# Attention in two-unit pairs: one shared output tile, one copy and one division for two heads' groups

## The reference

```python
q = (x @ Wq + bq).reshape(B, T, H, D)
kv_latent = jax.nn.gelu(x @ Wkd + bkd, approximate=False)
lat = kv_latent[..., :L] + kv_latent[..., L:]
kv = lat @ Wku + bku
k = kv[..., :C].reshape(B, T, H, D)
v = kv[..., C:].reshape(B, T, H, D)
attn = jnp.einsum('bqhd,bkhd->bhqk', q, k) * (1.0 / math.sqrt(D))
attn = jnp.where(causal, attn, -jnp.inf)
attn = jax.nn.softmax(attn, axis=-1)
out = jnp.einsum('bhqk,bkhd->bqhd', attn, v).reshape(B, T, C)
return out @ Wo + bo
```

## Time and profile before

| | |
|---|---|
| runs | 657.80, 651.72, 657.49 us; median 657.49 |
| profiled execution | 652.23 us, its span 650.4 us |
| mean granted TensorE clock | 0.966 of full speed |
| busy share of the span | PE 91%, DVE 84%, ACT 75%, weight loads 67%, POOL 26% |

### The profile page before, as it was taken

One profiled execution on the slowest core, in us unless ns is written; L12 is line 12 of the kernel. 1 busy time (PEld: TensorE's weight loads), 2 busy tenths in 40 slices (PEclk: granted clock), 3 DMA queues, 4 the chain that ended last, 5 costly groups with the idle time before them and its releaser, 6 DMA issues.

```text
span 650.4 us, 10963 instructions
## 1 busy us (share of the span) xinstructions
PE 594.2 (91%) x3276; PEld 435.8 (67%) x3276; DVE 545.8 (84%) x1344; ACT 488.0 (75%) x860; POOL 167.8 (26%) x143
## 2 busy tenths in 40 slices
PE   8888889888999999999999999791998999999995
PEld 5465556555546688888888887350575788888884
DVE  3868888888858868988888887769898789999997
ACT  4648999999647899999999998697735566666663
POOL 4323223223304043554355433031432000000000
PEclk9789999999998999999999999996897899999999
DMA  7000000000100032102210200000000132222201
GB/s 250 1 1 2 2 3 1 1 0 1 34 1 0 18 150 98 75 24 98 97 74 23 97 24 1 1 25 1 0 1 1 35 125 89 90 89 90 89 1 65
DMA packets 6490, 28.81 MB, mean 44 GB/s; under 512 B 862, under 2 KB 990, under 8 KB 4383
## 3 DMA queue, kind: packets, MB, share of 16 engines
q1 hardware_dynamic: 6448, 28.32, 12.1%
HBM read 27.13 MB, written 1.19 MB: 44 GB/s over the span
## 4 chain that ended last, share of the span: by engine, by line
PE 61%; DVE 27%; ACT 5%; issue 5%; DMA 1%; POOL 0%; DVEq 0%; SPq 0%; ACTq 0%; POOLq 0%
PE PS L1192 16%; PE PS L1193 16%; PE PS L1194 16%; DVE STAT L865 9%; PE PS L1338 2%; PE PS L1293 2%; PE PS L1205 2%; DVE RA L885 2%; PE PS L1218 2%; DVE SU L891 1%; DVE HL L680 1%; PE PS L1307 1%; DVE HN L668 1%; ACT RA L617 1%; DVE AR L1151 1%
## 5 line engine op out<-in xcount | busy, mean ns | idle before, releaser
L1006 DVE TENSOR_TENSOR RA<-AR,RA 128x512 fp32r<-128x512 f32 x144 | 137.9, 980 | 27.4 <-ACT RA L516 25.9
L515 ACT ACTIVATE AR<-PS,BI 128x512 f32<-128x512 f32 x144 | 99.6, 691 | 17.9 <-PE PS L1194 10.5
L1192 PE MATMUL PS<-HH,WH 128*128 128x512 f32 x272 | 109.4, 402 | 0.1
L1194 PE MATMUL PS<-HL,WH 128*128 128x512 f32 x272 | 107.2, 394 | 0.0
L1193 PE MATMUL PS<-HH,WL 128*128 128x512 f32 x272 | 107.0, 394 | 0.0
L516 ACT ACTIVATE RA<-PS,BI 128x512 fp32r<-128x512 f32 x144 | 98.6, 685 | 0.0
L865 DVE CUSTOM_DVE_ANT_0 STAT<-PS,MQ 128x128 f32<-128x128 f32 (+1 forms) x256 | 76.3, 354 | 20.0 <-PE PS L1294 19.9
L1192 PE MATMUL PS<-RA,WH 128*128 128x512 f32 x208 | 82.4, 396 | 3.2 <-DVE RA L1158 2.0
L1193 PE MATMUL PS<-RA,WL 128*128 128x512 f32 x208 | 81.0, 389 | 0.0
L1194 PE MATMUL PS<-RA,WH 128*128 128x512 f32 x208 | 81.0, 389 | 0.0
L313 POOL TENSOR_TENSOR AR<-AR 128x512 f32<-128x512 f32 x32 | 51.1, 1597 | 112.1 <-DVE AR L818 112.1
(11 more groups left out here) (212 smaller groups left out, 1165.8 us busy)
## 6 DMA issues: line engine op xcount, KB each, us to landing
AR<-comb SPq DMA_DIRECT2D x15, 1024.0 KB, 4.7
WS<-in_w SPq DMA_DIRECT2D x9, 512.0 KB, 5.5
WS<-in_w SPq DMA_DIRECT2D x8, 384.0 KB, 3.0
M<-in_mats SPq DMA_DIRECT2D x1, 1384.0 KB, 10.9
X<-in_xT SPq DMA_DIRECT2D x4, 256.0 KB, 4.2
out_xT<-X SPq DMA_DIRECT2D x4, 256.0 KB, 2.1
AR<-in_wmod SPq DMA_DIRECT2D x1, 768.0 KB, 8.1
KM<-in_kmats SPq DMA_DIRECT2D x1, 162.5 KB
```

The source lines that it names most:

```text
L515: act.activation(G[:, c, :], PS[:, c, :], ACT.Gelu_apprx_tanh, bias=bias).then_inc(s["act"], 1)
L1006: dve.tensor_tensor(out=GL[:, m0 % 2, c, :], in0=G[:, c, :], in1=f(GH[:, m0 % 2, c, :]), op=ALU.subtract).then_inc(s["lo"], 1)
L1192: pe.matmul(out, wh, xh, start=first, stop=False)
L1194: return pe.matmul(out, wh, xl, start=False, stop=last)
```

## The change

Units go in pairs, `pair = n // 2`. The even unit's `values` starts the accumulation in the head's 32 rows. The odd unit's uses a window of the value tile that begins eight columns earlier (`- 8 * odd`), so that its output lands in rows 8 to 15 and its sum in row 24, and accumulates onto the same tile. `evac_out`, `spread_sum`, `recip` and `divide` run once for each pair, with the same 128x256 shapes. `ON` and `Wo` have two groups for four, so that `out_proj` is two matmuls for four. `PR` has four buffers for two; `LAT`, `VALL`, `PR` move in `AR`. The input `mats` shrinks from 1384 to 1256 KB.

The steps are ordered anew. `values` runs for unit `n-2` in place of `n-1`; in even steps it stands where it stood, at the end. In odd steps `values(n-2)` and `project(n+3)` change places. ACT's copy of a pair stands behind `exps(n)` of an odd step, its `recip` in the next even one. DVE has `spread_sum` in even steps and `divide` in odd ones.

```diff
-            def evac_out(n, n0):
-                act.wait_ge(pv_done, n + 1)
-                if n0 >= 2:
-                    act.wait_ge(on_done, n - 1)
+            def evac_out(pair, pair0):
+                act.wait_ge(pv_done, 2 * pair + 2)
+                if pair0 >= 2:
+                    act.wait_ge(on_done, pair - 1)
...
-                if n0 >= 2:
-                    evac_out(n - 2, n0 - 2)
                 exps(n, n0)
+                if n0 >= 3 and n0 % 2 == 1:
+                    evac_out((n0 - 3) // 2 + 4 * it, (n0 - 3) // 2)
                 if n0 + 3 < UNITS:
                     evac_proj(n + 3, (n0 + 3) % 4)
-                if n0 >= 2:
-                    recip(n - 2, n0 - 2)
+                if n0 >= 4 and n0 % 2 == 0:
+                    recip((n0 - 4) // 2 + 4 * it, (n0 - 4) // 2)
...
-                dve.stream_shuffle(SU[:, n0 % 2, :], OT[:, n0 % 2, :], [16] * 32).then_inc(su_done, 1)
+                dve.stream_shuffle(SU[:, pair0 % 2, :], OT[:, pair0 % 2, :], ([16] * 8 + [24] * 8) * 2)\
+                   .then_inc(su_done, 1)
...
-                if n0 >= 3:
-                    divide(n - 3, n0 - 3, it)
-                if n0 >= 2:
-                    spread_sum(n - 2, n0 - 2)
+                if n0 >= 4 and n0 % 2 == 0:
+                    spread_sum((n0 - 4) // 2 + 4 * it, (n0 - 4) // 2)
+                if n0 >= 5 and n0 % 2 == 1:
+                    divide((n0 - 5) // 2 + 4 * it, (n0 - 5) // 2, it)
...
-                if n0 >= 1:
-                    pe.wait_ge(ot_done, n)
-                if n0 + 2 < UNITS:
-                    pe.wait_ge(qm_ready, n + 3)
-                own = [slice(32 * (4 * (n0 % 4) + j), 32 * (4 * (n0 % 4) + j) + 32) for j in range(4)]
+                odd = n0 % 2
+                if n0 >= 2 and not odd:
+                    pe.wait_ge(ot_done, n0 // 2 + 4 * it)
+                if n0 + 3 < UNITS and not odd:
+                    pe.wait_ge(qm_ready, n + 4)
+                own = [slice(32 * (4 * (n0 % 4) + j) - 8 * odd, 32 * (4 * (n0 % 4) + j) - 8 * odd + 32)
+                       for j in range(4)]
...
-                for g in range(4):
+                for g in range(2):
                     mm = pe.matmul(PS[:, 6, :], mat("wo", g), ON[:, g, t * BLK:(t + 1) * BLK],
...
+            def maxima_t(n, n0, it):
                 pe.wait_ge(mp_ready, 2 * n + 2)
-                if n0 >= 3:
-                    pe.wait_ge(ot_done, n - 2)
+                if n0 >= 4 and n0 % 2 == 0:
+                    pe.wait_ge(ot_done, (n0 - 2) // 2 + 4 * it)
...
-                if n0 + 3 < UNITS:
-                    project(n + 3, n0 + 3, it)
-                else:
-                    out_proj(n0 - 29)
+                if n0 % 2 == 0:
+                    project_next(n, n0, it)
+                elif n0 >= 3:
+                    values(n - 2, n0 - 2, it)
                 if n0 + 1 < UNITS:
-                    maxima_t(n + 1, n0 + 1)
+                    maxima_t(n + 1, n0 + 1, it)
                 if n0 + 2 < UNITS:
                     scores(n + 2, n0 + 2, 0)
-                if n0 >= 1:
-                    values(n - 1, n0 - 1, it)
+                if n0 % 2 == 1:
+                    project_next(n, n0, it)
+                elif n0 >= 2:
+                    values(n - 2, n0 - 2, it)
```

More of the change, by code:

```diff
@@ L886, in with_max, with spread_sum, divide @@
                    .then_inc(qm_ready, 1)
-            def spread_sum(n, n0):
-                if n0 == 0:
-                    dve.wait_ge(ot_done, n + 1)
-                dve.stream_shuffle(SU[:, n0 % 2, :], OT[:, n0 % 2, :], [16] * 32).then_inc(su_done, 1)
[L893 to L896, removed]
-                if n0 >= 1:
-                    dve.wait_ge(on_done, n)
-                dve.tensor_tensor(out=ON[:, n0 % 4, bass.ds((2 * it + n0 // 4) * SEQ, SEQ)],
-                                  in0=OT[:, n0 % 2, :], in1=SU[:, n0 % 2, :], op=ALU.mult).then_inc(on_done, 1)
+            def spread_sum(pair, pair0):
+                dve.wait_ge(ot_done, pair + 1)
+                dve.stream_shuffle(SU[:, pair0 % 2, :], OT[:, pair0 % 2, :], ([16] * 8 + [24] * 8) * 2)\
+                   .then_inc(su_done, 1)
+            def divide(pair, pair0, it):
+                dve.wait_ge(rsx_done, pair + 1)
+                if pair0 >= 1:
+                    dve.wait_ge(on_done, pair)
+                dve.tensor_tensor(out=ON[:, pair0 % 2, bass.ds((2 * it + pair0 // 2) * SEQ, SEQ)],
+                                  in0=OT[:, pair0 % 2, :], in1=SU[:, pair0 % 2, :], op=ALU.mult).then_inc(on_done, 1)
             def place_values(b, b0):
@@ L961, in _ @@
                 step(n)
-            divide(29, 29, 0)
-            spread_sum(30, 30)
+            spread_sum(14, 14)
             centre(1, 0)
             centre(1, 1)
-            divide(30, 30, 0)
-            spread_sum(31, 31)
+            divide(14, 14, 0)
+            spread_sum(15, 15)
             centre(1, 2)
-            divide(31, 31, 0)
+            divide(15, 15, 0)
             normalise(1, 0)
@@ L1316, in values @@
                 pe.wait_ge(vx_ready, 2 * (2 * it + n0 // 4) + 2)
[L1317 to L1321 removed]
+                odd = n0 % 2
[5 more added lines that the diff above has]
+                       for j in range(4)]
                 for j in range(4):
                     pe.matmul(PS[32 * j:32 * j + 32, 7, 0:256], VX[:, n0 // 4 % 2, 0, own[j]],
[L1324 removed]
+                              PR[:, n0 % 4, j, 0:256], start=not odd, stop=False)
                 for j in range(4):
                     mm = pe.matmul(PS[32 * j:32 * j + 32, 7, 128:256], VX[:, n0 // 4 % 2, 1, own[j]],
[L1327 removed]
+                                   PR[:, n0 % 4, j, 256:384], start=False, stop=bool(odd))
                 mm.then_inc(pv_done, 1)
             def out_proj(t):
[L1332 removed]
+                pe.wait_ge(on_done, 4 * t + 4)
                 if t == 0:
@@ L1336, in out_proj, with project_next @@
                     pe.wait_ge(y_scaled, 2 * t)
-                for g in range(4):
+                for g in range(2):
                     mm = pe.matmul(PS[:, 6, :], mat("wo", g), ON[:, g, t * BLK:(t + 1) * BLK],
-                                   start=(g == 0), stop=(g == 3))
+                                   start=(g == 0), stop=(g == 1))
                 mm.then_inc(wo_done, 1)
-            def maxima_t(n, n0):
+            def project_next(n, n0, it):
+                if n0 + 3 < UNITS:
+                    project(n + 3, n0 + 3, it)
+                else:
+                    out_proj(n0 - 29)
+            def maxima_t(n, n0, it):
                 pe.wait_ge(mp_ready, 2 * n + 2)
-                if n0 >= 3:
-                    pe.wait_ge(ot_done, n - 2)
+                if n0 >= 4 and n0 % 2 == 0:
+                    pe.wait_ge(ot_done, (n0 - 2) // 2 + 4 * it)
                 for q in range(2):
@@ L1390, in _ @@
             keep_clock(8)
-            maxima_t(0, 0)
+            maxima_t(0, 0, 0)
             scores(1, 1, 0)
@@ L1408, in _ @@
             mean(1, 1)
+            values(30, 30, 0)
             values(31, 31, 0)
```

45 lines of the change are left out of this document (21 added, 24 removed).

## The result

| | before | after |
|---|---|---|
| median | 652.64 us (5 runs, 651.27 to 657.80) | 719.48 us (5 runs, 713.29 to 730.26) |
| profiled execution, span | 652.23, 650.4 us | 719.48, 717.7 us |
| mean granted TensorE clock | 0.966 | 0.848 |

The changed kernel is slower by 9.5%: ratio 1.0946, 95% interval 1.0878 to 1.1014 (its two slowest runs of the five, 728.90 and 730.26, are left out of the ratio). The forecast was 670 us, its range ended at 678. Nearly all of the 67.3 us between the two spans lies in the attention. Step 1 starts at 45.52 for 45.18 (0.3 us), step 29 at 235.24 for 169.79 (65.1 us for those 28 steps), the last division comes 26.91 us later for 24.99 (1.9), and from there to the end it is 455.55 for 455.62.

What follows compares the result with a forecast made beforehand. A ring of waits between DVE and PE, 4.39 us a step, was taken as the bound. Longer steps add 17.9 us, the tail saves 3.1: net +14.8 on 655.7 gives 670 us, range 657 to 678.

Steps and rivals of the forecast that it cites:

- the clock: Rival: in the attention PE idles longer and drops to half clock, 1.4 us more a step, up to 710 us; chance 0.04.
- the sum: Attention loop to step 29: 142.6 us against 124.6, +17.9; with the tail, net +14.8 us.
- ring: Attention loop: DVE and PE wait for each other through scores, maxima and transposes, setting the ordinary step of 4.39 us.
- my waits: Attention loop: transposes wait for ACT's copy in odd steps (+0.53 us); DVE's cast waits for POOL's `join` in even (+0.91).
- odd step: Attention loop: ACT's copy behind both `exps` delays the transposes to T+2.75; step 4.92 us, 0.53 more.
- T: Time mark in each attention step: PE's load of the second half of `scores`.
- even step: Attention loop: late `project` moves POOL's `join` to 1.56 us after T, holding DVE's cast; step 5.30 us, 0.91 more.
- The doubt that I drew from the Trainium skill: Even steps: a cast is excluded only in a two-port mode, so L876 might slip through; 0.21 us less each.
- removed work: Attention loop: halved copies, Ln, Exp, shuffles and divisions, about 0.4 us each, lie off the ring; counted as nothing.
- tail: From step 29 to the last division: halved `out_proj` and one round less save 3.1 us.
- The base of 655.7: Mean of the three runs of the kernel before, in us, to which the net +14.8 us was added.

Runs made afterwards that it cites:

- together_plain: Changed kernel, both `values` of a pair ending the even step, `project` in its old place, copy ahead of `exps`, no filler matmuls: 696.53 us, ratio 1.0647.
- copy_late: Kernel before, nothing paired, only ACT's copy of the output tile moved behind the `exps` of its step: 676.05 and 713.89 us.
- values_together: `together_plain` plus three unread 128x512 matmuls at the end of each odd step: 655.68 us for 652.85, ratio 1.0023.
- fill_both: Changed kernel plus three unread 128x512 matmuls ahead of the transposes in both odd and even steps: 680.95 us, ratio 1.0470.
- fill_even: Changed kernel plus three unread 128x512 matmuls ahead of the transposes in even steps only: 689.74 us, one run.
- fill_odd: Changed kernel plus three unread 128x512 matmuls ahead of the transposes in odd steps only: 684.37 us, one run.
- fill_first: Changed kernel plus three unread matmuls ahead of the transposes in steps 3 to 11 only: 711.89 us, ratio 1.0881.
- copy_first: Changed kernel, odd steps with `values` ahead of `scores_t` and copy ahead of `exps`, `project` still late, filler matmuls in even steps: 665.78 us, ratio 1.0182.
- project_back: Changed kernel, odd steps with `project` in its old place, `values` behind it, copy behind `exps`, filler matmuls twice in odd steps: 674.58 us, ratio 1.0317.
- half_out: Kernel before with only `out_proj` halved, leaving out the second half of the head groups: 651.63 us for 652.85, ratio 0.9975.

## Why the prediction was wrong

**The step that failed** is the price of the rival *the clock*: the sum puts it at nothing, and its chance rests on "The gaps that I add are under 1 us each, so 0.04". The gaps are as small as that, 0.80 and 0.77 us for the weight loads, 0.40 and 0.50 for the matmuls, and the clock falls all the same. The kernel before, at a clock of 1.00, has matmul gaps as long (its timeline):

```profile
151.00 0.64 PE L1323 MATMUL PS<-AR 128*32 128x256 f32 x8 [0.60 <-DVE RA L885]
```

So a single gap was the wrong thing to look at. What the runs show is how full PE was over the steps, at a clock of 1.00: 17.54 of 20 us before, kept; 8.68 of 10.26 (changed kernel), 7.68 of 9.16 (`together_plain`, with gaps up to 1.3 us) and 8.24 of 10 (`copy_late`, one execution of two), lost; 9.85 of 10.53 and 8.66 of 9.16 with fillers, kept. That matmuls put into PE's waits keep the clock, and that a longer ring need not lose it, is shown by `values_together` and `together_plain`, with equal steps at full clock and 41 us between them, and by `fill_both`, whose steps are longer than the changed kernel's first ones and whose clock stayed through the loop in the profiled execution.

These shares draw no line, though: at 17.59 of 20 us `fill_even` kept the clock, at 17.63 `fill_odd` lost it once. There is chance in it too: ahead of step 3 the changed kernel and its four filled versions run the same instructions, and in two of the five executions (`fill_even`, `fill_first`) the clock fell at about 50 us. Nor is it shown what in the fillers holds it. They fill time, but they are also matmuls of 128 rows by 512 columns, longer than those of the loop, and no run separates the two.

The kernel before could have warned. It runs eighteen of the same idle matmuls (`keep_clock`) ahead of its loop, and PE already stood still for 2.46 of 20 us, which I read only as "no engine is full"; both of my waits add to it. The Trainium skill names a case of the kind (TensorE: Matmul & The Clock Gate, section A second HAM failure mode: psum-queue depth-cycling): in a kernel with matmuls of 512 columns, short pauses between groups of matmuls made the clock go back and forth. `together_plain` does so; the changed kernel falls once and stays down for 170 us.

**Where the 67 us went.** With its full-clock steps throughout (4.38 for step 1, fourteen of 5.23, thirteen of 5.07, the mean of 5.10 and 5.03) the changed kernel would need 143.5 us from step 1 to 29, an estimate from these rows; it took 189.7. So 18.9 of the 65.1 us are the two waits and 46.2 the clock. The rival's own price, 1.4 us a step, was right for even steps (6.72 for 5.30) and half of it for odd ones (7.80 for 4.92), because at half clock `scores_t` and `values` end later than the `exps` and so enter the ring.

**The odd step** was right in its cause and a little short in size: 5.03 to 5.10 for 4.92, transposes at T+2.87 for 2.75, since the `exps` begin at T+0.99 for T+0.91. `copy_first` shows the cause: with the copy early, odd steps are 4.63, of which some 0.24 is what `values` ahead of `scores_t` cost. So the copy behind the `exps` costs 0.4 (5.03 against 4.63) to 0.7 (5.10 against 4.39), and 0.6 to 0.75 in `copy_late`, for 0.53.

**The even step** was right: 5.23 to 5.32 for 5.30, the join at T+1.50 for 1.56. `project_back` shows the cause, since with `project` in place casts are 0.17 and even steps 4.39. The doubt that I drew from the Trainium skill (SBUF — State Buffer, section Who interferes with whom), that a cast is kept out only in a two-port mode, is settled for this cast by measurement: 128x8 with an output stride of 32 elements, and held for 1.01 to 1.12 us in every second step of all kernels with the late `join`, until just after the `join` ends. Whether the cast runs in such a mode, no run shows.

**The removed work** is worth nothing in the loop, as predicted: `values_together` has half the copies, Ln, Exp, shuffles and divisions and neither wait, and its pairs take 9.16 for 8.90. Its odd steps take the 4.39 of before; the 0.26 more is in the even step, which holds two `values`.

**The tail.** At full clock the last division comes 22.54 us after step 29 in `fill_both` (214.12 - 191.58) and 22.18 in `copy_first` (206.13 - 183.95), for 24.99 before: 2.5 to 2.8 gained, for 3.1 forecast. In the changed kernel itself that is lost: at half clock one `out_proj` is about as long as before (3.78 us for 3.60), and the tail is 1.9 longer. Whether a gain in this place reaches the end differs: from the last division to the end it is 455.9 us in `copy_first`, as before (455.6), but 458.3 in `fill_both`; and of the 3.7 us of `half_out` the medians show 1.2, and their interval ends at 3.5.

**Sum.** With the clock held the arithmetic comes near: `fill_both` in its profiled execution took 674.22 for 652.23, +22 where +14.8 was forecast. Of the 7 us between, thirteen odd steps of 5.20 for 4.92 make 3.6, of which the fillers add 0.17 a step, and 2.7 are lost again behind the tail. The base of 655.7 was 3 us too high, as later medians of the kernel before are 652 to 654, and the range's upper end is 677 by its own terms (657.8 + 17.9 + 1.3), not 678; neither decides anything.

**What stays open:** what in PE's work decides whether the clock falls. Where the other runs of `fill_both` lost it no trace shows, but by their mean clocks they did: 0.938 to 0.954, for 0.964 in the profiled one. The same holds for `copy_late`, 0.957 in one run and 0.847 in the other. No version beat the kernel before: the best, without either wait and with the clock held, is within 0.5% of it, and `half_out` leaves little to win in the tail.

## What to carry to other kernels

Before adding a wait to a loop that PE shares, look at how full PE is over whole steps and not at the longest gap: a change that only makes it wait can cost more by the clock (46 us here) than by the wait (19). The runs here give no share of busy time from which on the clock is safe. When a time is far beyond the sum of its waits, read the granted clock by windows first; a few matmuls that nothing reads, put where PE waits, tell clock from dependency in one run, and here gave back 38 of the 67 us. Merging small work off the critical path brought nothing here, and the order that the merging forced (a copy behind its last producer, a join at another place) was its price.

## What the runs showed of the hardware

I had not expected that the clock falls with PE busy 8.68 of 10.26 us and its matmuls never standing still for more than 0.63, about as long as in the kernel before (0.60). Nor that it stays at 0.50 for 170 us with PE's rows busy 19.50 of 20 us, where it came back by itself in `together_plain` at much the same busy share (18.70 of 20). At 0.50 the DVE cast that waits for POOL takes nearly as long as at 1.00 (1.10 us for 1.02), while a matmul group's time nearly doubles (`out_proj` 3.78 us, 1.98 at full clock).
